# A scan-and-experts layer on one core: the first chunk's products shared with GpSimd, its sums made by TensorE

## What is computed

```python
xs = silu(conv3(xc)); dt_param, Bp, Cp = split(xs @ W_x.T)
dt = softplus(dt_param @ W_dt.T + b_dt) + 1e-5
A_disc = exp(-exp(A_log) * dt[..., None])          # decay, per channel and state
Bx = Bp[:, :, None, :] * dt[..., None] * xs[..., None]
s = A_t * s + Bx_t ; ssum_t = s.sum(-1)            # over time; sum over 16 states
y = (Cp @ W_C.T) * ssum + D_param * xs ; out = (y @ W_out.T) * silu(z)
```

## Time and profile before

| | us |
|---|---|
| median of 3 runs | 1182.86 (1182.24 to 1186.41) |
| the profiled execution's own time | 1181.82 |
| its span, first to last instruction | 1180.0 |
| busy in the span: PE / DVE / ACT / POOL | 1018.0 / 662.9 / 641.0 / 685.3 |
| scans of the first chunk | 34.47 to 92.99 |
| mean granted TensorE clock | 0.907 |

### The profile page before, as it was taken

How to read it: one execution, slowest core, us unless ns; L and a number is a source line. 1 busy time by engine, 2 the same in 40 slices (tenths; PEclk the granted TensorE clock), 3 DMA queues, 4 the chain that set the end, 5 groups by cost and what they waited for, 6 DMA issues and landing times.

```text
span 1180.0 us, 15468 instructions
## 1 busy us (share of the span) xinstructions
PE 1018.0 (86%) x4682; PEld 821.4 (70%) x4682; DVE 662.9 (56%) x1159; ACT 641.0 (54%) x1238; POOL 685.3 (58%) x670
## 2 busy tenths in 40 slices
PE   7437597878977878988969899799999999999997
PEld 4213275656655656766757788689999999998886
DVE  7999999899997888877975332000000000100333
ACT  5776778787586686876672533133333333333342
POOL 0797867769489987799796447532343333322221
PEclk9657597888987988999989999899999999999999
DMA  8210100202002016143474583698999989863521
GB/s 290 65 36 0 50 23 18 72 1 90 1 19 72 1 40 230 37 121 79 107 207 132 164 273 61 157 286 245 339 351 329 310 270 270 268 183 63 170 72 53
DMA packets 141635, 163.91 MB, mean 139 GB/s; under 512 B 26344, under 2 KB 126976, under 8 KB 141536
## 3 DMA queue, kind: packets, MB, share of 16 engines
q1 hardware_dynamic: 125872, 144.20, 37.8%
q0 software_dynamic: 15680, 18.72, 8.3%
HBM read 136.57 MB, written 26.74 MB: 138 GB/s over the span
## 4 chain that ended last, share of the span: by engine, by line
PE 51%; POOL 20%; issue 12%; DVE 8%; ACT 5%; DMA 1%; SPq 1%; DVEq 0%; POOLq 0%; ACTq 0%
PE psum L1164 22%; PE psum L1131 11%; POOL Ssum L1805 11%; PE psum L1120 6%; PE psum L1143 6%; DVE S L1372 3%; POOL list_d L1824 3%; ACT A L1662 1%; DVE psum L1347 1%; PE psum L1086 1%; POOL gb L1813 1%; PE psum L1107 1%; POOL scale L1736 1%; DMA bb<-b 1%; POOL xs L1780 1%
## 5 line engine op out<-in xcount | busy, mean ns | idle before, releaser
L1805 POOL TENSOR_TENSOR Ssum<-Ssum,S 128x512 f32<-128x512 f32 x240 | 302.9, 1285 | 68.1 <-DVE S L1372 67.1
L1164 PE MATMUL psum<-w,hT 128*128 128x256 f32 x1136 | 253.7, 381 | 7.0 <-issue 5.6
L1855 POOL DMA_INDIRECT acc_d<-y,ID x71 | 112.8, 1589 | 222.6 <-DMA acc_d<-y,ID 121.5
L1164 PEld LDWEIGHTS psum<-w,hT 128*128 128x128 f32 x1136 | 214.6, 191 | 36.9 <-issue 6.7
L1662 ACT ACTIVATE A<-dts,nea 128x512 f32<-128x512 f32 x256 | 175.1, 718 | 42.6 <-DVE S L1372 31.2
L1131 PE MATMUL psum<-XT,w 128*128 128x256 f32 x800 | 184.7, 388 | 14.7 <-DMA bb<-b 6.9
L1347 DVE TENSOR_TENSOR psum<-us,psum 128x512 f32<-128x512 f32 x256 | 163.4, 683 | 37.3 <-PE psum L1050 37.2
L1131 PEld LDWEIGHTS psum<-XT,w 128*128 128x128 f32 x800 | 153.9, 194 | 42.5 <-issue 12.3
L1372 DVE TENSOR_TENSOR_SCAN S<-A,carry,psum 128x512 f32<-128x512 f32 x120 | 148.2, 1264 | 0.0
L1372 DVE TENSOR_TENSOR_SCAN S<-A,psum 128x512 f32<-128x512 f32 x120 | 141.1, 1204 | 0.7 <-POOL Ssum L1805 0.7
L1701 ACT ACTIVATE hT<-psum,bb 128x256 f32<-128x256 f32 x200 | 83.3, 472 | 94.4 <-PE psum L1131 94.2
(11 more groups left out here) (176 smaller groups left out, 1285.3 us busy)
## 6 DMA issues: line engine op xcount, KB each, us to landing
w<-W SPq DMA_DIRECT2D x92, 1024.0 KB, 6.4
bb<-b SPq DMA_DIRECT2D x46, 128.0 KB, 8.4
xnb<-x SPq DMA_DIRECT2D x16, 256.0 KB, 3.2
Xr<-x SPq DMA_DIRECT2D x16, 256.0 KB, 5.0
x_d<-gb SPq DMA_DIRECT2D x8, 512.0 KB, 2.9
xn_d<-nb SPq DMA_DIRECT2D x8, 512.0 KB, 3.2
X<-x_d SPq DMA_DIRECT2D x16, 256.0 KB, 7.5
ACC<-acc_d SPq DMA_DIRECT2D x16, 256.0 KB, 5.3
```

What stands on the lines that cost most here:

```text
L1164: t = eng.matmul(bank(g)[:, 256 * k:256 * k + 256], hT[n % 2][:, f, 128 * k:128 * k + 128], w[:, f, :], start=f == 0, stop=f == 7)
L1805: eng.tensor_tensor(to, to, of, ALU.add).then_inc(nsum, 1)
L1855: eng.indirect_dma_start(acc_d, bass.IndirectOffsetOnAxis(ap=ID[:, col, 1:2].bitcast(u32), axis=0), y[n % NY][:, k, :], None, compute_op=A ...
```

## The change

In the first chunk, for the 12 states of `BYPOOL` (2 to 5 and 8 to 15), the product of half 1 is made by GpSimd (new step "product"), in place in SBUF (`Bx`, over the expert weights' room). B comes there by transfers: chunk 0's B rows are stored to DRAM (`b_d`) and read back spread over 128 partitions in four transfers, issued by SP at dbc_out. VectorE then makes only half 0's product, in place in the spread's bank. The decays of half 1 of these states stand in PSUM, in `UB` for even n and in a bank lent from the five for odd n, and are queued at most three steps ahead. The sum over the states is made by TensorE (step "total"), by matmuls with the identity that add up in two PSUM banks; ScalarE copies them out (total_out) in the second chunk. GpSimd keeps the seven sums of half 1 for n = 1 to 7. post(0) starts three steps later. On SP the weight and table loads, the wait for `got_s` and the preset of acc_d move from before the loop to behind the spreads, ahead of load_x of chunk 1. The first fetches of expert weights wait for the first chunk's scans. The semaphores got_l become one.

```diff
+BYPOOL = [2, 3, 4, 5, 8, 9, 10, 11, 12, 13, 14, 15]
+EARLY = 8
...
+    lent, sums = -1, (-2, -3)
     def decay_until(m):
         while decayed[0] < min(m, 32 * NC):
+            if decayed[0] < 32 and in_psum(decayed[0]) and decayed[0] > m - AHEAD - 1 + 3:
+                return
             say("decay", *divmod(decayed[0], 32))
...
     def main(i):
         if i == 0:
+            say("lend", lent)
             say("spread", 0, 0)
         for k in range(32):
             m = 32 * i + k
+            if i == 0:
+                if k % 2 == 0 and k // 2 + 2 in BYPOOL:
+                    say("product", k // 2 + 2)
+                if k >= 3 and not (k % 2 == 0 and k - 3 < 2 * EARLY):
+                    say("total", k - 3, sums[(k - 3) % 2])
+                if k == 18:
+                    say("total", 1, sums[1])
+            elif i == 1 and k < 4:
+                if k == 0:
+                    say("unlend", lent)
+                if k < 3:
+                    say("total", 29 + k, sums[(29 + k) % 2])
+                if k > 1:
+                    say("total_out", k - 2, sums[k - 2])
...
     def post(i):
         late = i == NC - 1
+        if i == 0:
+            for _ in range(3):
+                yield
...
+def in_psum(m):
+    return m % 2 == 1 and m // 2 in BYPOOL
...
+        def decay_bank(n):
+            return bank(LENT) if n % 2 else UB
...
                     if m >= 2:
-                        eng.wait_ge(scan, 2 * (m - 1))
+                        eng.wait_ge(scan, 2 * (m - 1) - (m - 2 in BYPOOL))
...
+                elif step == "total":
+                    k, g = a
+                    if k < 2:
+                        take(g)
+                    if k == 1:
+                        eng.wait_ge(nsum, EARLY - 1)
+                    eng.wait_ge(scan, k + 1)
+                    t = eng.matmul(bank(g), ident, S[:, (k - 2) % NS, :] if k > 1 else S0[0][k],
+                                   start=k < 2, stop=k >= 30)
...
+                    if i == 0 and n in BYPOOL:
+                        eng.tensor_tensor(bb, us[0][:, 0, :], bb, ALU.mult).then_inc(mult, 2)
+                        continue
...
-                    eng.wait_ge(mult, m + 1)
+                    pooled = i == 0 and n in BYPOOL
+                    if pooled and c:
+                        eng.wait_ge(product, BYPOOL.index(n) + 1)
+                        factor, term = decay_bank(n), Bx[:, n - 2, :]
+                    else:
+                        eng.wait_ge(mult, m + 1)
+                        factor, term = A[m % NA], BB[(m // 2) % 2] if c or pooled else UB
...
+                    if m < 32 and in_psum(m):
+                        to = decay_bank(n)
...
+                        eng.wait_ge(scan, 2 * n - 2 + (n - 1 not in BYPOOL))
+                    elif m >= NA:
                         eng.wait_ge(scan, m - NA + 1)
...
+                elif step == "product":
+                    n, = a
+                    if n == BYPOOL[0]:
+                        eng.wait_ge(u_done, 2)
+                    if n in (2, 4, 8, 12):
+                        eng.wait_ge(got_b[(2, 4, 8, 12).index(n)], 16)
+                    eng.tensor_tensor(Bx[:, n - 2, :], us[0][:, 1, :], Bx[:, n - 2, :], ALU.mult).then_inc(product, 1)
...
-                    if n:
+                    if n and (i or c and n < EARLY):
...
-            eng.dma_start(wout, W_outT.rearrange("(c p) e -> p c e", p=128)).then_inc(got_wo, 16)
...
             for step, *a in PLAN:
                 if step == "load_x":
                     load_x(*a)
+                elif step == "dbc_out" and a[0] == 0:
+                    eng.wait_ge(dbc_out, 1)
+                    eng.dma_start(b_d, dbc[0][0:16, :]).then_inc(st_b, 16)
+                    eng.wait_ge(st_b, 16)
+                    for k, (n, w) in enumerate([(2, 2), (4, 2), (8, 4), (12, 4)]):
+                        eng.dma_start(Bx[:, n - 2:n - 2 + w, :], b_d[n:n + w, :].unsqueeze(0).to_broadcast([128, w, TC])
+                                      ).then_inc(got_b[k], 16)
+                    eng.dma_start(wout, W_outT.rearrange("(c p) e -> p c e", p=128)).then_inc(got_wo, 16)
+                    eng.dma_start(wg, gate_wT.rearrange("(c p) e -> p c e", p=128)).then_inc(got_wo, 16)
+                    eng.dma_start(s1, sW1.rearrange("(c p) f -> p c f", p=128)).then_inc(got_s, 16)
+                    eng.dma_start(s2, sW2.rearrange("(c p) h -> p c h", p=128)).then_inc(got_s, 16)
+                    eng.dma_start(sb1t, sb1).then_inc(got_s, 16)
+                    eng.dma_start(sb2t, sb2.unsqueeze(0).to_broadcast([128, D])).then_inc(got_s, 16)
+                    eng.dma_start(VAL, vals.rearrange("p (n w) -> p n w", w=3)).then_inc(got_val, 16)
+                    eng.dma_start(list_d, pads).then_inc(padded, 16)
+                    eng.wait_ge(got_s, 64)
+                    eng.dma_start(rows8(acc_d[TC * LATE:, :]), sb2t.unsqueeze(1).to_broadcast([128, (T - TC * LATE) // 128 + 1, D])
+                                  ).then_inc(acc_set, 16)
```

More of the change, by code:

```diff
@@ L604, in finishing @@
     say("last_result", 1)
-TAKING = {"xT", "nT", "xc", "z", "dbc", "dt", "cmat", "wout", "logit", "top2", "count", "turn", "up", "down"}
-GIVING = {"xT_out", "nT_out", "xc_out", "z_out", "dbc_out", "dt_sum", "yadd", "gated", "lg_out",
+TAKING = {"lend", "total", "xT", "nT", "xc", "z", "dbc", "dt", "cmat", "wout", "logit", "top2", "count", "turn", "up", "down"}
+GIVING = {"unlend", "total_out", "xT_out", "nT_out", "xc_out", "z_out", "dbc_out", "dt_sum", "yadd", "gated", "lg_out",
           "place", "turn_out", "up_out", "down_out", "weighed"}
@@ L641, in emptied @@
         return ("xc_out", taps(i, n)) if i else ("conv", 2 * n + 2)
+    if step == "lend":
+        return "scan", 32
+    if step == "total":
+        return "total_out", i % 2 + 1
     if step == "dbc":
@@ L677, in banks @@
             if at in last:
-                before[g], turns[g] = EMPTIED[last[at]], turns[last[at]] + 1
+                before[g], turns[g] = EMPTIED[last[at]], turns[last[at]] + (step != "lend")
             else:
-                before[g], turns[g] = ("scan", 32 * NC) if at >= NGEN else None, 1
+                before[g], turns[g] = ("scan", 32 * NC) if at >= NGEN else None, int(step != "lend")
             where[g], last[at] = at, g
@@ L689 @@
 BANK, TURN, BEFORE = banks()
+LENT = next(row[1] for row in PLAN if row[0] == "lend")
+TOTALS = [row[1] for row in PLAN if row[0] == "total"]
 NTH = {group: n for n, group in enumerate(GROUPS)}
@@ L732, in build @@
     ALU, ACT, AX = mybir.AluOpType, mybir.ActivationFunctionType, mybir.AxisListType
+    b_d = nc.dram_tensor("b_d", [16, TC], f32, kind="Internal").ap()
     x1_d = nc.dram_tensor("x1_d", [T, D], f32, kind="Internal").ap()
@@ L837, in build @@
         at[0] = weights
+        Bx = nc.alloc_sbuf_tensor_at("Bx", [128, 14, 512], f32, offset=weights + 4096).ap()
         hx, hxT = put("hx", [128, 256]), put("hxT", [128, 2, 8])
@@ L881, in build @@
         u_done = sem("u_done")
+        st_b, got_b, product = sem("stored_b"), [sem(f"got_b{k}") for k in range(4)], sem("product")
+        totalled, total_out = sem("totalled"), sem("total_out")
         spread, decay, mult, scan, nsum = sem("spread"), sem("decay"), sem("mult"), sem("scan"), sem("nsum")
@@ L897, in build @@
         st_y, st_sh = ([sem(f"stored_{k}{i}") for i in range(NY)] for k in "ys")
-        got_l = [sem(f"got_l{i}") for i in range(NC)]
+        got_l = sem("got_l")
         got_acc = [sem(f"got_acc{i}") for i in range(NC)]
@@ L1358, in _ @@
                             j, last = divmod(s - NS, 30)
+                            if j == 0:
+                                e = last + 2
+                                if e >= 30:
+                                    eng.wait_ge(total_out, e - 29)
+                                elif e in TOTALS:
+                                    eng.wait_ge(totalled, TOTALS.index(e) + 1)
+                                else:
+                                    eng.wait_ge(nsum, added_by_pool(0, e))
                             if j % 2 == 0:
@@ L1371, in _ @@
                         first = 0.0
[L1372 removed]
+                    eng.tensor_tensor_scan(to, factor, term, first,
                                            ALU.mult, ALU.add).then_inc(scan, 1)
@@ L1659, in _ @@
                             eng.wait_ge(statd[1], 2 * 5)
-                    if m >= NA:
-                        eng.wait_ge(scan, m - NA + 1)
-                    eng.activation(A[m % NA], dts[i % 2][:, c, :], ACT.Exp, scale=nea[:, c, n:n + 1]).then_inc(decay, 1)
+                    to = A[m % NA]
+                    if m < 32 and in_psum(m):
+                        to = decay_bank(n)
+                        if n % 2 and BEFORE[LENT] is not None:
+                            name, value = BEFORE[LENT]
+                            eng.wait_ge(emptying[name], value)
```

(13 more changed lines are left out.)

36 lines of the change are left out of this document (18 added, 18 removed).

## The result

| | before | after |
|---|---|---|
| median, us | 1184.36 (1182.24 to 1186.41, 4 runs) | 1224.70 (1223.24 to 1226.75, 4 runs) |
| ratio | | 1.034, 95% interval 1.031 to 1.037 |
| span of the profiled execution | 1180.0 | 1222.0 |
| busy in the span: PE / DVE / ACT / POOL | 1018.0 / 662.9 / 641.0 / 685.3 | 1033.4 / 657.4 / 636.9 / 674.4 |

What follows compares the result with a forecast made beforehand. No engine was full over the span; VectorE bounds the first chunk, on which all later work hangs. 1181.8 + 11.0 (second chunk's later start) + 1.5 (third chunk) = 1194.3, 1195 against the median, range 1182 to 1206 us.

Steps and rivals of the forecast that it cites:

- VectorE's gain per state: First chunk: a pooled state takes 2.93 us instead of 3.41, a gain of 5.8 us over 12 states.
- GpSimd hidden: First chunk: GpSimd keeps up, 2.6 us per state against VectorE's 2.93; product 2 made by about 40.5, wanted at 42.0.
- When x lands: SP queue, first chunk: chunk 1's x, issued behind spreads, loads and acc_d, is there at 53.3 us; wanted at 39.27.
- Rivals 1 and 3: Spread of B nearly free, 1186 us, chance 0.11; or at half rate, x at 62.2, 1204 us, chance 0.10.
- Scan 5: First chunk, VectorE: scan 5 waits for decay 5 behind chunk 1's normalisation, starting at 56.0 instead of 42.4, 13.6 us late.
- 2.6 and 2.2 us of waits for TensorE: First chunk after scan 5: VectorE waits 2.6 us for transposes, sum and spread, then 2.2 until the projections are through.
- the 0.7 us for ScalarE: First chunk: allowance for ScalarE's 6.5 us silu block with table loads and for later short lookahead.
- Their order changes, and this decides: ScalarE, first chunk: only decays 0 to 4, not 0 to 8, precede chunk 1's normalisation; late x makes decay 5 late.
- So the tail is not longer; I charge 1.5 us: Later chunks: post(0)'s five calls move into the third chunk, idle planner steps 23 to 27 absorb them; 0 to 4 us.
- the offset then stays until the end: Expected sign: after the second chunk's first scan near 104, the delay stays until the end, third chunk a little longer.
- Rival 2: x not held back, landing before about 41: second chunk at 90.0, 1181 us, or 1177 with warm TensorE; chance 0.09.

Runs made afterwards that it cites:

- e6: Kernel before plus only the change's store, spreads and order on SP, which nothing uses, so chunk 1's x comes late: ratio 1.0104 to before.
- e1: Changed kernel with post(0)'s pace worked out from its real length, three more in the second chunk: ratio 1.0115 to before.
- e4: Kernel before with nothing but three idle steps at the head of post(0): ratio 1.0285 to before.
- e3: Changed kernel with post(0)'s pace from its real length and SP's loads moved behind chunk 1's x: ratio 1.0015 to before.
- e5: Kernel before, unchanged, run again for a profile on the chip of these runs: ratio 0.9994.
- e8: e3 with five filler matmuls on TensorE ahead of chunk 1's transposes and state 0's sum said at step 5, not 3: ratio 0.9988 to before.
- e10: Kernel before with the change's transfers as in e6, chunk 1's preparation placed over steps 8 to 27 instead of 0 to 27: ratio 1.0027 to before.
- e11: e8 with the last sums and their copies one step earlier and post(0) two idle steps behind, not three: ratio 0.9962 to before, 1180.34 us.
- e12: e11 with one idle step for post(0) instead of two: ratio 0.9965 to before.

## Why the prediction was right or wrong, point by point

- **VectorE's gain per state: right.** 2.93 forecast, 2.96 measured. A dependence was put at 0.11 and costs 0.12: in the changed kernel the scan starts 79.42 - 78.71 = 0.71 behind the product that it reads, where two independent products start 0.59 apart. The Trainium skill (VectorE: DVE Perf Modes, The DRAIN you can't avoid) found on eight copies that a semaphore behind each costs nothing extra; that does not carry over to these operations, of which the second waits for the first.
- **GpSimd hidden: right.** Its first product ran from 39.21 to 40.47, forecast by 40.5; VectorE never waited for one.
- **When x lands: right.** Forecast 53.3 (its terms, 44.6, 7.1 and 1.5, give 53.2), and ScalarE began at 51.94; the wait for s1 and s2 ended at 43.26, forecast 44.6. The spread of B was no dearer and no cheaper than a load: the queue moved 376 GB/s from 27 to 43 us, against the 354 that I took. Rivals 1 and 3 are out by this.
- **Scan 5: right.** 56.0 forecast, 54.69 measured. After it 2.6 and 2.2 us of waits for TensorE, measured 2.42 and 1.46; TensorE's clock came up as forecast (four records of 512 columns, 3.75 us at the low clock, take 1.88 from 59.21 on), and the 0.7 us for ScalarE did not appear. Second chunk at 104.0 forecast, at 101.8 measured.
- **"Their order changes, and this decides": wrong.** The normalisation's place among the decays is what scan 5 waited for, but e6 has the old order and waits longer. The same late x also holds the head of TensorE's queue, and there the spread of the next state but one is behind it. I had that wait as an addition of 2.6 us; it was a second wall at nearly the same place, and in e6 it gives the 12 us by itself. No run has the decays' wait without it.
- **"So the tail is not longer; I charge 1.5 us": wrong, and this is the miss.** I saw that post(0)'s logits would move from step 26 behind the end of the second chunk and that five calls would go into the third, and then took the planner's idle calls from step 23 to 27 as room in which the lag is made up. It is not made up. The calls at a chunk's head are held back by the banks that post and prep have, so the five late pieces do not shift by five calls but to behind that hold, the gelu lands at step 13 of the third to the sixth chunk instead of step 8, and the next pair starts from there again. Charged 1.5 us, measured 33 in the changed kernel; undone by e1 (27), reproduced by e4 (34). The sign "the offset then stays until the end" failed with it: 8.8 us at the second chunk, 42.0 at the end. Two prices were missing: the gelu ahead of dbc_out (6.9 us for TensorE's queue in the third chunk, 6.6 in the fourth), and the expert work left for a tail that TensorE fills (22 us).
- **Rival 2, x in time, 1177 to 1181:** e3 is that case with the lag taken out: 0.15% slower than before. The 3 us ahead at the second chunk are there (89.4 against 92.5 in e5), and they are lost in the second and third chunk, where I charged 1.5. (The rival's 1177 leaves that 1.5 out; with it the sum is 1178.6.)

## What to carry to other kernels

When a hand-paced order of work is changed, follow each moved step to the end of the program, in the order of work itself, and not only to the next gap that looks like room: a step later by one became a lag that a whole program carried, for 26 us. And when a transfer becomes late, look at every queue in which a user of it stands ahead of someone else's work; the fix is to move the user down (12.5 us to 3) or the transfer up. Time saved in one stage is worth what the next stages let through: of the 4.9 us that e8 saves in the first chunk, 0.5 are left two chunks later.

## What the runs showed of the hardware that was not expected

- The kernel before differs from chip to chip by some 0.3 to 0.4% in its median, and in the profiles most of it lies in one stage. From the eighth chunk to the end, with the same 3083 TensorE records, it takes 620.4 us in the first profile and 620.4 to 623.5 on the chip of e10, e11 and e12; on the chips of e1 and e3 and of e5 to e8 it takes 626.9 to 629.0. These are single executions, and the two of the kernel before lie 7.2 us apart where its medians are 3.6 to 4.2 apart. Only ratios on one chip are safe at this size.
- A scan with its decay in PSUM and its product in SBUF takes 1.20 us, as with the two the other way round (1.20 to 1.22), and beside GpSimd's two-operand products (1.25 to 1.28 us, as its sums take in the kernel before) neither engine became slower.
